# Attention probabilities regrouped in aligned blocks of 32 by 10 transfers instead of 13, with three half buffers, half of the heads scaled on ScalarE and the expert rows mixed in on GpSimd

## The reference, cut to what matters

```
h = rms(x, ln1_w[l])
q, k, v = h @ wq[l], h @ wk[l], h @ wv[l]          # rotated by position: q, k
scores = q @ k.T / 8 + causal_bias
attn = softmax(scores)                             # 112 x 112 per head, 16 heads
x = clip(x + (attn @ v) @ wo[l], -100, 100)
h = rms(x, ln2_w[l])
probs = softmax(h @ wr[l]); top 2 of 8 experts, their weights made to sum to 1
out = sum over the 2 experts e of weight_e * (silu(h @ wg[e]) * (h @ wu[e])) @ wd[e]
x = clip(x + out, -100, 100)
```

## Time and profile before

| | us |
|---|---|
| Median of three executions | 2311.7 |
| The profiled execution | 2303.1 |
| its span, first to last instruction | 2301.3 |
| TensorE busy | 1887.7 (82%) |
| VectorE busy | 1432.4 (62%) |
| ScalarE busy | 840.8 (37%) |
| GpSimd busy | 551.5 (24%) |
| Mean granted TensorE clock | 0.903 |

### The profile page before, as it was taken

The page is one execution under the profiler, slowest core; times in us unless marked ns, Lnnn a source line. Parts: engine busy times, 40 slices in busy tenths (PEclk is TensorE's granted clock), DMA queues, the critical chain, the costliest instruction groups (busy, mean ns, idle before and its releaser), DMA issues.

```text
span 2301.3 us, 36337 instructions
## 1 busy us (share of the span) xinstructions
PE 1887.7 (82%) x10100; PEld 1359.7 (59%) x10101; DVE 1432.4 (62%) x3173; ACT 840.8 (37%) x3369; POOL 551.5 (24%) x724
## 2 busy tenths in 40 slices
PE   7987788689996777689997786769997777759996
PEld 6876666456665565555665665545665565635663
DVE  4766667554576667654466767745466676764456
ACT  5544444322224444332224444332223444342221
POOL 4741111420122121412032222222022221132004
PEclk9998888799997888899998888889999888879998
DMA  5324421346634431336653432235663433134666
GB/s 162 108 76 137 120 81 38 113 115 146 167 78 137 129 107 37 96 84 152 149 144 95 133 107 65 54 104 136 148 159 90 127 114 97 36 81 129 144 158 167
DMA packets 290238, 260.11 MB, mean 113 GB/s; under 512 B 157474, under 2 KB 238068, under 8 KB 289972
## 3 DMA queue, kind: packets, MB, share of 16 engines
q1 hardware_dynamic: 275752, 222.50, 36.5%
q0 software_dynamic: 13952, 35.33, 5.3%
q10 hardware_dynamic: 380, 0.38, 0.1%
HBM read 137.32 MB, written 73.05 MB: 91 GB/s over the span
## 4 chain that ended last, share of the span: by engine, by line
PE 47%; SPq 26%; DVE 15%; DMA 8%; issue 3%; POOL 0%; ACT 0%; DVEq 0%; POOLq 0%; ACTq 0%
SPq L412 25%; PE ps L978 18%; PE ps L1006 10%; PE ps L917 7%; DMA probT<-tarena 6%; DVE tarena L1687 4%; DVE parena L1671 3%; PE ps L842 2%; PE ps L860 2%; PE ps L925 1%; PE ps L972 1%; PE ps L786 1%; PE ps L824 1%; DVE x_sb L1693 1%; PE ps L851 1%
## 5 line engine op out<-in xcount | busy, mean ns | idle before, releaser
L978 PE MATMUL ps<-arena,xeT 128*128 x1120 | 509.2, 594 | 0.0
L1311 ACT ACTIVATE parena<-ps,nmax 112x112 f32<-112x112 f32 x1024 | 344.7, 387 | 137.9 <-DVE nmax L1657 133.1
L628 POOL TENSOR_TENSOR qk<-qk,rope 128x448 f32<-128x448 f32 x128 | 145.6, 1137 | 851.6 <-DVE rope L1641 851.6
L978 PEld LDWEIGHTS ps<-arena,xeT 128*128 128x128 f32 x1120 | 211.1, 191 | 198.2 <-issue 191.9
L860 PE MATMUL ps<-xnT,wqk_s 128*128 128x224 f32 x1280 | 269.2, 360 | 14.8 <-DVE rope L1641 10.4
L925 PE MATMUL ps<-cst,x_sb 112*128 112x112 f32 x128 | 38.4, 398 | 287.0 <-DVE x_sb L1694 287.0
L860 PEld LDWEIGHTS ps<-xnT,wqk_s 128*128 128x128 f32 x1280 | 238.2, 192 | 26.0 <-DVE rope L1641 11.7
L1687 DVE STREAM_TRANSPOSE tarena<-parena 128x1024 f32<-128x1024 f32 x128 | 159.1, 1243 | 148.7 <-DMA probT<-tarena 147.3
L1358 ACT ACTIVATE parena<-ps,er 128x512 f32<-128x512 f32 x140 | 96.2, 687 | 416.2 <-PE ps L978 416.2
L1311 ACT ACTIVATION_READ_ACCUMULATOR parena<-ps,nmax 112x1 f32 x1024 | 246.2, 240 | 0.0
L607 POOL DMA_INDIRECT y_in<-sorted_y,pos x114 | 109.7, 963 | 555.3 <-DMA sorted_y<-tarena 389.6
(11 more groups left out here) (210 smaller groups left out, 2927.9 us busy)
## 6 DMA issues: line engine op xcount, KB each, us to landing
probT<-tarena SPq DMA_DIRECT2D x832, 56.0 KB
sorted_y<-tarena SPq DMA_DIRECT2D x140, 128.0 KB
...
hid_d<-tarena SPq DMA_DIRECT2D x240, 64.0 KB
...
```

The source lines that it names most:

```text
L628: pool.tensor_tensor(q, q, rope[m % 2][:, :], ALU.add).then_inc(g_rope, 1)
L978: last = pe.matmul(ps[:, bank, :], xeT[u][:, k, :], w[:, bass.ds(e * 1024 + k * 512, 512)], start=(k == 0), stop=(k == KD - 1))
L1311: last = act.activation(prob[0:S, :, n, 0:KW], ps[0:S, bank, h * S:h * S + S].rearrange("q (j k) -> q j k", j=KB), ACT.Exp, bias=nmax[:, b ...
```

## The change

Parts of it:

- Keys stay in their natural order, 112 contiguous, and are cut in blocks of 32, 32, 32 and 16. `BLOCKS` has the 10 pairs with j not above i. Each transfer moves 32 partitions (16 in the last block) in two pieces of 1 KB per partition, one for each half of the heads, where it moved 28 partitions with one piece of 2 KB.
- `xnT`, `v_s`, `prob` and the query and value products lose the padding; products that ran over 128 rows run over 112. `turned` becomes three half buffers: the first half of sample b goes to buffer b % 2, the second always to buffer 2. The first transpose waits for the landing of sample b-2's transfers, the second for that of sample b-1's.
- VectorE scales heads 0 to 7 only. Heads 8 to 15 are scaled on ScalarE by 8 instructions (`scale_probs`), which wait for the reciprocals (`d_sum`); the second transpose waits for them (`a_norm`).
- `rows_in` moves from VectorE (three instructions) to GpSimd (five).
- The scratch of the squares and three zeroing instructions at the start change place or size.

On VectorE, in layer 1: the stretch from one transpose of the first half on, before. L1687 is the transpose, L1610 to L1617 are `rows_in`, L1693 and L1694 `add_attention`.

The diff, cut to its core:

```diff
-KB, KW = 4, S // 4
+KB = 4
 QB = 4
 PAD = 32
-TNP = PB * KB * PAD
-BLOCKS = [(i, j) for i in range(QB) for j in range(KB) if KW * j <= min(PAD * i + PAD, S) - 1]
-SELF_SCALED = 0
+KP = KB * PAD
+BLOCKS = [(i, j) for i in range(QB) for j in range(i + 1)]
...
-        parena = sb("parena", [128, KB * NH * PAD])
-        prob = parena[:, :].rearrange("q (j n k) -> q j n k", j=KB, n=NH)
-        tarena = sb("tarena", [128, KB * NH * PAD])
-        turned = tarena[:, :].rearrange("k (j n q) -> k j n q", j=KB, n=NH)
+        v_s = sb("v_s", [S, GB, NKV * HD])
+        parena = sb("parena", [128, NH * KP])
+        prob = parena[:, :].rearrange("q (n k) -> q n k", n=NH)
+        tarena = sb("tarena", [128, 3 * KB * 8 * PAD])
+        turned = tarena[:, :].rearrange("k (c j n q) -> k c j n q", c=3, j=KB, n=8)
...
-                    sp.dma_start(probT[PAD * j:PAD * j + KW, i, :, :], turned[PAD * i:PAD * i + KW, j, :, :]).then_inc(ld_pt, 16)
+                    n = min(PAD, S - PAD * j)
+                    sp.dma_start(probT[PAD * j:PAD * j + n, i, :, :].rearrange("k (p n) q -> k p (n q)", p=2),
+                                 turned[PAD * i:PAD * i + n, b % 2:3:2 - b % 2, j, :, :].rearrange("k p n q -> k p (n q)")).then_inc(ld_pt, 16)
...
-            def scale_probs(l, b, p):
-                pool.wait_ge(d_sum, l * 2 * SELF_SCALED + 2 * b + p + 1)
-                heads_p = prob[0:S, :, 8 * p:8 * p + 8, 0:KW]
-                pool.tensor_tensor(heads_p, heads_p, bc(bc(rrec[:, 8 * p:8 * p + 8], 1, [S, KB, 8]), 3, [S, KB, 8, KW]),
-                                   ALU.mult).then_inc(g_norm, 1)
+            def rows_in(l, b):
+                pool.wait_ge(gathered[b % 2], (l - 1) * (16 * TOPK * B // 2) + (b // 2 + 1) * 16 * TOPK)
+                row = x_sb[:, b, 0:D]
+                for k in range(TOPK):
+                    y = y_in[:, b % 2, k, :]
+                    eps(pool.tensor_scalar(y, y, wts[:, b, k:k + 1], None, ALU.mult))
+                    ins = pool.tensor_tensor(row, row, y, ALU.add)
+                    if k == 0:
+                        eps(ins)
+                ins.then_inc(d_yr, 1)
+                pool.wait_ge(d_yr, l * B + b + 1)
+                pool.tensor_scalar(row, row, CLIP, -CLIP, ALU.min, ALU.max).then_inc(d_x, 1)
...
-                    if b < SELF_SCALED:
-                        scale_probs(l, b, 0)
                     if more:
                         add_rotated(l, g + 1, 4 if odd else 1)
-                    if b < SELF_SCALED:
-                        scale_probs(l, b, 1)
+                    if l and b + LEAD < B:
+                        rows_in(l, b + LEAD)
                     if more and not odd:
...
+            def scale_probs(l, b):
+                act.wait_ge(d_sum, l * B + b + 1)
+                for n in range(8, NH):
+                    last = act.activation(prob[0:S, n, 0:S], prob[0:S, n, 0:S], ACT.Copy, scale=rrec[:, n:n + 1])
+                last.then_inc(a_norm, 1)
...
+                    scale_probs(l, b)
...
                 def sums(b, p):
                     dve.wait_ge(a_exp, l * 32 + 2 * b + p + 1)
                     hs = slice(8 * p, 8 * p + 8)
-                    if b < SELF_SCALED:
-                        if b:
-                            dve.wait_ge(g_norm, l * 2 * SELF_SCALED + 2 * b + p - 1)
+                    if p:
                         dve.reciprocal(rrec[:, hs], rsum[:, b % 2, hs]).then_inc(d_sum, 1)
                     else:
                         step(dve.reciprocal(rrec[:, hs], rsum[:, b % 2, hs]))
-                        step(dve.tensor_tensor(prob[0:S, :, hs, 0:KW], prob[0:S, :, hs, 0:KW],
-                                               bc(bc(rrec[:, hs], 1, [S, KB, 8]), 3, [S, KB, 8, KW]), ALU.mult))
+                        step(dve.tensor_tensor(prob[0:S, hs, 0:S], prob[0:S, hs, 0:S], bc(rrec[:, hs], 2, [S, 8, S]), ALU.mult))
 
                 def turn_probs(b, p):
 
-                    if b < SELF_SCALED:
-                        dve.wait_ge(g_norm, l * 2 * SELF_SCALED + 2 * b + p + 1)
+                    if p:
+                        dve.wait_ge(a_norm, l * B + b + 1)
                     if b:
-                        dve.wait_ge(ld_pt, (l * B + b) * 16 * len(BLOCKS))
+                        dve.wait_ge(ld_pt, (l * B + b - 1 + p) * 16 * len(BLOCKS))
                     elif l:
                         for u in range(2):
                             dve.wait_ge(st_ye[u], l * 16 * TILES[u] + 16)
@@ -1684,8 +1691,8 @@
                         for u in range(2):
                             dve.wait_ge(st_ye[u], 16)
                     hs = slice(8 * p, 8 * p + 8)
-                    dve.transpose(turned[:, :, hs, :].rearrange("k j n q -> k j (n q)"),
-                                  prob[:, :, hs, :].rearrange("q j n k -> q j (n k)")).then_inc(d_turn, 1)
+                    dve.transpose(turned[:, 2 if p else b % 2, :, :, :],
+                                  prob[:, hs, :].rearrange("q n (j k) -> q j n k", j=KB)).then_inc(d_turn, 1)
...
                     sums(b, 0)
                     if more:
                         rotate(step, l, g + 1, 4 if odd else 1, 4 if odd else 5)
-                    if b >= SELF_SCALED:
-                        turn_probs(b, 0)
                     sums(b, 1)
-                    if l and b + LEAD < B:
-                        rows_in(step, l, b + LEAD)
                     if b > 2:
                         take_logits(b - 3)
                     if b > 1:
@@ -1925,8 +1928,7 @@
                         choose(0)
                     if b == MID_STEP:
                         choose(1)
-                    if b < SELF_SCALED:
-                        turn_probs(b, 0)
+                    turn_probs(b, 0)
```

37 lines of the change are left out of this document (16 added, 21 removed).

## The result

The changed kernel takes 1971.53 us (median of four executions, 1968.68 to 1978.09), the kernel before beside it 2309.87 us: a ratio of 0.8537, 95% interval 0.8511 to 0.8562. The forecast was 2055 us with a range of 1985 to 2170. The sign and the mechanism came as forecast, the size did not: the time lies 83 us under the forecast and 13 under the range. The profiled execution took 1970.95 us, its span is 1969.1.

The account below looks back on a forecast made before the run. It took a one-sample ring of waits, with regrouping issues 25% of the chain, as the bound, then TensorE. Attention stages fall from 1196.8 to 962.8 us: 2303.1 - 234 - 14 (after the last regroupings) = 2055 us, range 1985 to 2170.

Parts of the forecast that it names:

- The ring opens: Attention stages: the first transpose no longer waits for the previous landing; the queue's cycle falls from 20.7 to 10.4-13.4 us.
- TensorE is late next: Middle of a layer: TensorE, not the queue, bounds the steps, at 16.25 us in the mean.
- The failed step: TensorE's steps: 31.47 us busy in two, turn of x 0.65, product 3.2, giving steps of 15.1 and 17.4 us.
- the routing: Routing steps, where VectorE has more work: 3 us a layer, between 0 and 6.
- Rival 1: TensorE without stalls: ScalarE's scaling and routing cost nothing on the path, steps of 15.5 us, about 1995 us; chance 0.15.
- Issue: Regrouping transfers on SyncE: 0.45 us each, ten in 4.9 us, up to 7.9 at the dear end.
- Rival 3: Regrouping transfers cost by the piece: 1.70 us an issue, ten take 17.4, 2510 us; chance 0.06.
- ScalarE: Odd steps: eight scalings take 2.5 us and delay the copy of x, which the product's second half waits for.
- GpSimd: Layers 1 to 3: the moved row mixing takes 3.5 us, hidden; contention costs VectorE 0.2 us a step.
- rival 2: GpSimd contention or ScalarE's scalings stretch the ring of exponentials: about 2130 us, both and worse 2180; chance 0.16.
- Rival 4: Something else still holds the first transpose or turn of x behind the landing: 17.6 us a step, 2150 us; chance 0.06.
- Tail: After each layer's sixteenth regrouping, cheaper issues ahead of the last product: 3.5 us four times, 14 us less.

Follow-up runs that it names:

- e12: Kernel before with four dead matmuls a step on TensorE ahead of the turn of x: 2286.48 us, ratio 0.9891.
- e5: Changed kernel with both scalings on VectorE and none on ScalarE: 2171.06 us, ratio 0.9179.
- e4: Changed kernel with the mixing of the expert rows back on VectorE, behind the second reciprocal: 2102.98 us, ratio 0.8909.
- e7: Changed kernel with twenty transfers of one 1 KB piece per partition instead of ten of two: 2188.18 us, ratio 0.9461.
- e8: Changed kernel with one buffer, one 2 KB piece per partition and both transposes behind the same landing: 1976.64 us, one execution.
- e9: Changed kernel with ScalarE's copy of the turned x ahead of its scalings in odd steps: 2035.34 us, ratio 0.8608.
- e14: Changed kernel with ScalarE's copy ahead of its scalings in odd steps, repeated on another chip: 1967.79 us, ratio 0.8515.
- e13: Changed kernel as it is, companion on the chip of the repeated copy-order run: 1978.81 us, ratio 0.8572.

## Why the prediction was wrong in its size

- **The ring opens, TensorE is late next:** right. VectorE's wait for the landing (147.3 us, 59 times) is gone, the issues are down from 25% to at most 1% of the chain, and TensorE is busy 26.84 of 28.80 us in two steps.
- **The failed step: "It is busy 31.47 us in two steps, 15.7 a step", and "Turn of x 0.65, product 3.2", taken over into steps of 15.1 and 17.4.** These durations came from rows at a granted clock of 0.80, from an engine that had stood for up to 9.4 us ahead of the turn. The change takes that idle time away and the durations with it: busy 26.84 in 28.80. Step by step, even: the queries' third piece ends after 10.4 us instead of 11.2, then a wait of 0.64 for `add_attention` that I had not, turn 0.45 for 0.65, product 2.1 with its wait for 3.2. That is 13.5 for 15.1. Odd: values end at 11.0 for 11.9; ScalarE's copies and scalings take 3.4 behind them for 3.9; the half product is 0.98 for 1.6. That is 15.3 for 17.4. The mean is 14.4 where I had 16.25 to 16.45. TensorE's shorter work is 0.8 + 0.2 + 1.1 + 0.9 + 0.6 = 3.6 us of two steps, as large as the whole shortfall; ScalarE's gain of 0.5 and the unforeseen 0.64 about cancel. Over the kernel busy time fell by 81 us, and the forecast was 83 too high; that the two numbers are so alike proves nothing by itself; the steps do. In layer 1 the twelve intervals from the second regrouping to the fourteenth take 179.2 us, where 200.4 were forecast; at 14.4 a step they would be 172.8, so the routing took 6.4 us where I had 3. The first and the last two take 39.7 for 40.9.
- **It was shown from both sides.** With the idle time filled, the old kernel's product takes 1.74 us (`e12`); with VectorE later, the new kernel's takes 2.75 to 3.25 (`e5`, `e4`). The granted clock says it directly. In the kernel before, these are the stretch of the product that the forecast used, and the last product of layer 0, the same 16 matmuls (columns as in the earlier trace rows):

```profile
722.35:725.50 3.15, 3.15 (x18) 1.41 (x18) 2.07 (x3) 1.54 (x5) 2.01 (x2) 0.50 0.00 0
463.31:465.00 1.69, 1.69 (x17) 0.91 (x17) 0.00 (x0) 0.54 (x1) 0.00 (x0) 1.00 0.46 167
```

  A clock of 0.50 is the level of 1.2 GHz. How much idle time brings it down is not settled: in the kernel filled with four, products of 2.43 and 3.13 stood behind turns that had waited 2.40 and 2.27.
- **Rival 1 came nearest**, at 1995, and gave the clock as one reason, but still priced a step at 15.5 "a little under the 15.7 of busy time". The trace of before had the correction in it, in the last product of layer 0:

```profile
463.31 1.74 PE L917 MATMUL ps<-probT,v_s 128*64 128x384 f32 x16 [3.05 <-DMA probT<-tarena]
```

  It is 1.5 us under the row I used. In the forecast's own reckoning that is 1.5 us in the even step and 0.7 in the odd one, where only half of the product stands behind ScalarE's copy: 2.2 of the 3.7 us by which the forecast of a pair of steps was long. Most of the rest is in the scores and the turn, which were also read at 0.50.
- **Issue:** 0.597, not 0.45; ten in 6.35 us or more instead of 4.9. Hidden, as argued, so it cost nothing. That the piece is free and the shape counts was right; the hidden tiles' store was the wrong neighbour for the base price. Rival 3 falls with the 0.597, and `e7` and `e8` say why: a transfer of one piece costs the same as one of two.
- **ScalarE:** eight scalings 2.33 us (2.5 forecast), wait of the product 0.74 (0.9). Right, and the wait is what `e9` and `e14` take away.
- **GpSimd:** `rows_in` 4.1 to 4.4 us with its gaps (3.5): a scaling by a column of weights is 0.93 and not 0.5, the clip 0.40. The 0.2 us a step that I put for its contention do not show: in layer 1 the early steps are 14.4 us in the mean as in layer 0, where there is no `rows_in`. What I had at nothing is the new neighbour of the clip in `add_attention`: beside the rotation's addition it takes 0.85 instead of 0.29, in layer 0 too, on the path ahead of the turn. It is part of the 0.64 and 0.77 of waiting. A scaling took 2.5 beside two such GpSimd additions. The move pays 45 us (`e4`), far from rival 2.
- **Rival 4:** the waits show it false. **Tail:** 13.7 us for the four layers, 14 forecast. **Sums:** rival 2 adds up to 2141 us and not to 2130, which changes nothing here.

What the parts are worth, each taken back alone, in hundredths of the time before: 4.7 for the scaling on ScalarE, 2.0 for the rows on GpSimd, 1.6 for the order (with one landing wait), 0.3, not clear of noise, for the third buffer. They need not add up to the 12.9 of the whole on that chip, since each hides behind the others. Twenty issues instead of ten cost 8.9 (`e7` against the changed kernel of `e13`, on two chips of like speed). 13 issues of the old shape in the new order, with the rest of the change kept, were not tried.
